# Two unread products of the identity behind each tile's products in the first two edge loops of a four-layer graph network

## The reference, cut to what matters

```python
def _L0_gnn_ref(x, edge_index, W_l, b_l, W_r, gamma, beta):
    src, dst = edge_index[0], edge_index[1]
    agg = jax.ops.segment_sum(x[src], dst, num_segments=N)
    deg = jax.ops.segment_sum(jnp.ones_like(src, dtype=x.dtype), dst, num_segments=N)
    mean = agg / jnp.maximum(deg, 1.0)[:, None]
    out = mean @ W_l.T + b_l + x @ W_r.T
    ...
def _L1_gnn_ref(h, relvectors, w_ih, w_hh, b_ih, b_hh, edge_src, edge_dst, edge_rel):
    msg = h[edge_src] + relvectors[edge_rel]
    red = jax.ops.segment_sum(msg, edge_dst, num_segments=h.shape[0])
    return _gru_cell(red, h, w_ih, w_hh, b_ih, b_hh)
...
x = _layernorm(x + _L0_gnn_ref(x, edge_index, ...), axis=-1)
x = _layernorm(x + _L1_gnn_ref(x, L1_gnn_relvectors, ..., src, dst, edge_type_16), axis=-1)
```

## Time and profile before

| | |
|---|---|
| runs before | 8210.89 us median, 8205.14 to 8220.28 |
| the profiled execution: its own time | 8210.32 us |
| its span, first to last instruction | 8208.5 us |
| mean granted TensorE clock over the span | 0.782 of full speed |
| busy: PE, PE weight load | 5486.4 us (67%), 4033.4 us (49%) |
| busy: DVE, ACT, POOL | 5435.7 (66%), 2562.7 (31%), 3711.2 us (45%) |

### The profile page before, as it was taken

One profiled execution on the slowest core, in us unless ns is written; L12 is line 12 of the kernel. 1 busy time (PEld: TensorE's weight loads), 2 busy tenths in 40 slices (PEclk: granted clock), 3 DMA queues, 4 the chain that ended last, 5 costly groups with the idle time before them and its releaser, 6 DMA issues.

```text
span 8208.5 us, 116030 instructions
## 1 busy us (share of the span) xinstructions
PE 5486.4 (67%) x23622; PEld 4033.4 (49%) x23625; DVE 5435.7 (66%) x13161; ACT 2562.7 (31%) x9014; POOL 3711.2 (45%) x3988
## 2 busy tenths in 40 slices
PE   6365666526666666975555555799677777777798
PEld 4133333313433333434555555688455555555587
DVE  9767666766767664226655555675578777777666
ACT  1022222302222221112444444311345544545211
POOL 0267666536666662343555555200244444444211
PEclk8576676666667777986777777899788888888899
DMA  3232333323333331023333333355355454544411
GB/s 105 54 87 84 87 88 87 86 78 93 87 92 86 95 88 48 31 75 102 108 107 106 105 106 106 107 158 164 97 139 138 136 140 134 139 138 138 95 44 36
DMA packets 427643, 820.10 MB, mean 100 GB/s; under 512 B 75880, under 2 KB 275544, under 8 KB 426458
## 3 DMA queue, kind: packets, MB, share of 16 engines
q0 software_dynamic: 194048, 574.45, 25.2%
q1 hardware_dynamic: 230618, 231.98, 9.1%
q10 hardware_dynamic: 2304, 6.29, 0.3%
HBM read 692.86 MB, written 279.19 MB: 118 GB/s over the span
## 4 chain that ended last, share of the span: by engine, by line
PE 27%; DVE 17%; issue 10%; another core or an unknown queue 5%; SPq 3%; DMA 2%; ACT 1%; DVEq 1%; ACTq 1%; POOL 0%; POOLq 0%
PE ps L1482 4%; PE ps L1747 3%; DVE big L1417 3%; SPq L1340 2%; PE ps L1710 2%; PE ps L1936 2%; PE ps L1953 2%; DVE big L1840 2%; PE ps L831 2%; DVE big L1856 2%; DMA bas_d<-big 2%; PE ps L1432 2%; DVE big L1865 2%; DVE wreg L1828 1%
## 5 line engine op out<-in xcount | busy, mean ns | idle before, releaser
L831 PE MATMUL ps<-ring 128*128 x3528 | 1574.4, 578 | 1114.1 <-issue 478.5
L831 PEld LDWEIGHTS ps<-ring 128*128 128x128 f32 x3528 | 758.8, 266 | 1583.3 <-issue 1556.4
L1432 PE MATMUL ps<-big,ring 128*128 128x128 f32 x4928 | 885.2, 347 | 628.4 <-DVE big L1407 431.2
L745 POOL DMA_INDIRECT ring<-xl_d,idx x832 | 843.2, 1013 | 737.2 <-DVEq L640 316.3
L812 ACT CAST ring<-ohb 128x128 f32<-128x128 bf16 x1764 | 523.5, 298 | 2075.8 <-DVE ohb L775 1266.5
L1432 PEld LDWEIGHTS ps<-big,ring 128*128 128x128 f32 x4928 | 806.6, 251 | 707.0 <-DVE big L1407 486.5
L1368 POOL DMA_INDIRECT big<-x_d,idx x832 | 793.0, 953 | 790.6 <-ACT ring L1393 545.4
L1618 POOL DMA_INDIRECT ring<-kv_d,gidx x754 | 712.7, 945 | 841.5 <-issue 758.3
L745 POOL DMA_INDIRECT ring<-x_d,idx x832 | 825.9, 993 | 443.3 <-issue 225.4
L785 DVE TENSOR_TENSOR big<-big,ps 128x257 f32 (+1 forms) x1764 | 754.6, 428 | 259.1 <-issue 187.8
L1417 DVE SCALAR_TENSOR_TENSOR big<-big,ps 128x256 f32<-128x256 f32 x1232 | 590.1, 479 | 369.1 <-DMA bas_d<-big 210.1
(11 more groups left out here) (408 smaller groups left out, 9157.4 us busy)
## 6 DMA issues: line engine op xcount, KB each, us to landing
bas_d<-big SPq DMA_DIRECT2D x1232, 128.0 KB
att_d<-wreg SPq DMA_DIRECT2D x464, 132.0 KB
big<-bas_d SPq DMA_DIRECT2D x49, 1024.0 KB, 5.6
x_d<-ring SPq DMA_DIRECT2D x147, 128.0 KB, 1.7
ring<-xl_d,idx POOLq DMA_INDIRECT x832
ring<-x_d,idx POOLq DMA_INDIRECT x832
big<-x_d,idx POOLq DMA_INDIRECT x832
kv_d<-ring SPq DMA_DIRECT2D x49, 260.0 KB, 2.3
```

The lines of the kernel that those rows point to most:

```text
L745: nc.gpsimd.indirect_dma_start(out=rows[:, j, :], out_offset=None, in_=table, in_offset=bass.IndirectOffsetOnAxis(ap=idx_of(c), axis=0)).t ...
L831: T.matmul(ps[k][:, 0:D], ohf[:, k, :], rows[:, slot, :].rearrange("p a d -> p (a d)"), start=True, stop=True)
L1432: last = nc.tensor.matmul(ps[j % 8][:, 0:FW].rearrange("p (n h b) -> p n h b", n=NB, h=H)[:, :, h, :], xs[:, j, h * P:(h + 1) * P], wts[:, ...
```

## The change

Behind the two products of each tile, and behind the signal `mm`, PE makes two f32 products of the identity with itself. They go into ps7, which neither loop uses or reads.

```diff
@@ -835,6 +835,8 @@
                     last = T.matmul(ps[k][:, D:D + T16], ohb[:, k, :], t16oh[:, bass.ds(of[a], 1), :].rearrange("p a t -> p (a t)"),
                                     start=True, stop=True)
                 last.then_inc(e["mm"], 1)
+                for k in range(2):
+                    T.matmul(ps[7][:, k * P:(k + 1) * P], ident[:, :], ident[:, :], start=True, stop=True)
             walk(pe, NQ, U1, 0, step, flat=True)
```

## The result

The changed kernel takes 8291.45 us (8284.49 to 8295.15, 4 runs) against 8208.01 us for the kernel before beside it (4 runs): a ratio of 1.0101, 95% interval 1.0085 to 1.0117, or 83 us more. The profiled execution has a span of 8293.1 us, 84.6 more than before.

A forecast was written before the change was run, and what follows sets the result against it. No engine was full: PE, DVE and POOL hold each other in a ring, POOL nearest a floor. Longer tiles +84 us and shorter waits -41 us, net +43 on 8210, gave 8253 us; 8-in-10 range 8150 to 8390.

The forecast's parts named there:

- the likeliest case: Whole kernel slightly slower through the two edited loops: net +43 us, range 8226 to 8322 us; chance 0.45.
- the sum of the prediction: Both loops: +84 us for longer tiles and -41 us for shorter waits, net +43 us, giving 8253 us.
- The price of the products: PE in both loops: with two added products a tile takes 1.02 us at the high clock, 1.98 at the low.
- The cost, 835 tiles each 0.10 us longer: Both loops: 35.1% of 2538 us is PE's pace, 835 tiles at 1.067 us; at 1.167 each, +84 us.
- the chain's share of L831: L831, a PE product in the loops, has 35.1% of the 473 us from 2655 to 3128; applied to both loops.
- The return, 221 waits each 0.52 us sooner at the high clock, -41 us: POOL's 107 + 114 waits for `mm` in both loops shorten as the high clock's share rises from 0.38 to 0.74.
- the signs of the prediction: Expected in both loops: clock 0.82 to 0.89, about 20 us longer each, POOL's waits for `mm` longer by as much.
- A wait like this isn't for PE's speed, and a busier PE changes nothing in it as long as its work still ends before.: Said of loop 1's standstill at 735 us: no PE work from 735.37 to 740.20, DVE waiting 4.88 us.
- The work was hidden: Rival: the added 423 us fits into the 476 us PE idles in a loop; 8211 us, chance 0.18.
- The much slower case: Rival: standstills keep both loops' clock at 0.69, a tile takes 1.46 us, +117 us a loop, 8444 us; chance 0.12.
- The Trainium skill's rule: Matmul bursts too short for the waits between them throw PE back to its low clock each time.
- its faster case: Rival: loops' clock well above 0.905, tiles behind waits announced sooner; 8100 us, or 8155 with half on the path; chance 0.25.

## Why the prediction was right, and where it was not

- **Direction and range.** Slower, by 83 us where I said 43; inside my range for the likeliest case (8226 to 8322). This is in good part luck: with the measured price and clock the sum of the prediction gives no loss at all, as the next points show.
- **The price of the products.** 0.99 us a tile high and 1.92 low, against 1.02 and 1.98. The clock is 0.89 in both loops, against 0.87. Both steps hold, and that PE stays under the loop's length holds too: 1056 of 1310 us, 81% busy.
- **The cost, 835 tiles each 0.10 us longer.** The size came out near the truth, the reasoning did not. With the measured 0.99, 1.92 and 0.89 (high for 78% of the time) the mean is 1.11 us and the term is +34 us instead of +84; for one product it is about -110, where +35 was measured. The step that failed is to read the chain's share of L831 as tiles that PE paces at its mean rate.
- **The return, 221 waits each 0.52 us sooner at the high clock, -41 us.** No run shows this gain. With the measured clock it would be -46 us, and the whole sum 34 - 46 = -12 us, where +83 was measured. POOL's waits for `mm`, which the signs of the prediction had some 40 us longer in all, grew from 411 to 489 us. In five kernels the growth of these waits is the growth of the time: 33 and 35 us for one product, 78 and 83 for two, 86 and 89 for two ahead of the signal, 276 and 282 for four, 830 and 855 for the one-column products.
- **"A wait like this isn't for PE's speed, and a busier PE changes nothing in it as long as its work still ends before."** The first half fits the runs: in the change PE is faster, 0.89 against 0.69, and POOL's waits are longer, not shorter. The second half fails: for two products or more PE's own products are held up in a standstill, 217 us before L839 alone, so PE's work doesn't end before it. That added products are added delay for this reason is argued, not shown: for one product the idle time before L839 is 0.0 and for four it is 90 us, and the loss is there all the same.
- **The rivals.** The work was hidden on the chip of 7067 us: 0.9997 with POOL asking in pairs. No run with added products was clear of noise faster than its like without them, although there the clock reached 0.99: POOL's gathers are the pace, not PE. The much slower case was seen only in a kernel of another kind: with one-column products the clock was 0.50 and the time 9061 us, but no standstill kept the clock low there, as PE was busy all the time.
- **The Trainium skill's rule** (TensorE: Matmul & The Clock Gate, section "HAM oscillation — how this bites in real kernels") agrees with the rows of the change: more work between the waits, 0.69 to 0.89. It doesn't cover the one-column products, where PE had hardly a wait and the clock was 0.50; there the measurement decides. The time that the prediction drew from it, by the rule alone a tile at 1.02 us, is that of its faster case, the second in its list of rivals and not the third; no run shows that gain.

What stays open: what holds PE in a standstill, and how one product comes to cost 35 us. The idle time within PE's tiles shows in every profile of a kernel of 8200 us and more that has two or four of the 128-column products, and not on the chip of 7067 us; DVE's room and the place of the signal were varied and aren't it. Whether it needs the indirect gathers wasn't settled, since the plain DMAs ran on the chip that has none. Loading the added instructions is a rival that the pages speak against: the packets of the instruction queue q8 went from 228 to 283 in the change, but they are 283 too with the one-column products and with POOL asking in pairs, where the idle time before L839 is 4.9 and 0.0 us.

The packed traces hold one more clue, counted from their records of semaphore updates. The 832 gathers of loop 1 should leave 13312 of them (16 each); the trace of the kernel before has 2331, that of the same kernel with pairs, on the chip of 7067 us, 13277. Of the 882 updates of `mm` in loop 1 it is 738 and 882. In the changed kernel about nine in ten of the updates that the one-hots, casts, sums and small products should leave are there 10 to 12 us before PE stands still within a tile (87 places in loop 1), and about one in four in the last 3 us before; the run of it on the third chip shows the same. So the standstills and the missing records go together. Whether the signals themselves come late, or the recording of the profile is overrun and holds the engines, no run tells: every time here is of an execution that was recorded. For the same reason "issue" and "remote" are weak names in the profiles of 8200 us and more, where the record of what ended a wait may be one of the missing ones. L839 is not concerned: it waits for nothing.

## What to carry to other kernels

- Filler products can raise TensorE's clock (here 0.69 to 0.81, 0.89 and 0.97 with one, two and four of 128 columns; one-column ones had 0.50), but no run here shows them to pay. One product that made the mean tile shorter, as worked out above, made the loop longer. Before adding them, add up the waits of the engine with the highest floor (here POOL, 1047 us plus 195) and ask which of them PE's rate would end.
- Idle time in front of an instruction that waits for nothing is a reading worth looking for: it tells apart an engine that is late from one that is held.
- Compare kernels on one chip. The two products cost 1% beside a kernel before of 8208 us and beside one of 8219 us, and nothing on the chip of 7067 us, there with POOL asking in pairs.
- A name for what ended a wait is as good as the trace's records of the signals. Count how many of the expected ones are there before building on it.

## What the runs showed of the hardware

- The same kernel took 7067 us on one chip and 8205 and 8219 us on two others; the difference isn't only in these loops: they take 1087 and 1084 us there (with POOL asking in pairs) against 1267 and 1271, and what follows 4308 us against 5080. On the faster one no idle time within PE's tiles is left.
- PE can sit idle between the two records of one f32 product: 1.16 us from one start to the other, where both together take 0.60 in other tiles at the same clock.
- With one-column f32 products PE's weight loads were 81% busy, its products 100% by the profile, and the granted clock 0.50 in loop 1.
- Traces of one kernel differ by chip in what they record: 2331 of 13312 landing updates in loop 1 in the run of 8210 us, 13277 on the chip of 7067 us (there with pairs).
